# Cross-attention and MoE in one program on one core: the low-half matmuls moved last, VectorE's small steps moved behind the projection's sum, and two low halves moved behind the maxima

## The reference, cut to what matters

```python
q = (layernorm(x) @ Wq); k = context @ Wk; v = context @ Wv      # per head
attn = softmax(q @ k.T * SCALE)
x = x + (attn @ v) @ Wo + bo
h = layernorm(x)                      # then a routed MoE: 32 experts, top 4 of 2 groups of 4, and a shared one
x = x + mixed_experts(h) + shared(h)
```

## Time and profile before

| | |
|---|---|
| time, median of 3 runs | 3259.04 us (3258.24 to 3260.62) |
| the profiled execution's own time | 3257.45 us |
| its span, first to last instruction | 3255.6 us, granted clock 0.995 |
| attention's groups | to about 2952 us of the span; then the MoE |
| PE, DVE, ACT, POOL busy | 98%, 80%, 65%, 41% of the span |
| the chain that ended last | PE 85%, DVE 12% |

### The profile page before, as it was taken

The page is one execution under the profiler, slowest core; times in us unless marked ns, Lnnn a source line. Parts: engine busy times, 40 slices in busy tenths (PEclk is TensorE's granted clock), DMA queues, the critical chain, the costliest instruction groups (busy, mean ns, idle before and its releaser), DMA issues.

```text
span 3255.6 us, 39933 instructions
## 1 busy us (share of the span) xinstructions
PE 3185.7 (98%) x14510; PEld 2470.6 (76%) x14510; DVE 2619.5 (80%) x4840; ACT 2128.3 (65%) x2642; POOL 1327.1 (41%) x893
## 2 busy tenths in 40 slices
PE   7899999999999999999999999999999999999999
PEld 5677777777777777777777777777777777776787
DVE  5788888888888878888888888887888888888766
ACT  4566666666666666666666666666666666676555
POOL 4334433344334433344433434334433344225565
PEclk9999999999999999999999999999999999999999
DMA  2000000000000000000000000000000000115453
GB/s 82 6 27 11 15 22 6 27 11 27 11 22 11 27 11 11 22 11 27 11 27 6 27 11 11 27 6 27 11 27 11 22 11 11 50 26 115 112 131 76
DMA packets 52696, 93.13 MB, mean 29 GB/s; under 512 B 23699, under 2 KB 24468, under 8 KB 52116
## 3 DMA queue, kind: packets, MB, share of 16 engines
q1 hardware_dynamic: 52500, 90.58, 10.3%
HBM read 86.88 MB, written 2.88 MB: 28 GB/s over the span
## 4 chain that ended last, share of the span: by engine, by line
PE 85%; DVE 12%; issue 1%; ACT 1%; POOL 0%; DMA 0%; POOLq 0%; DVEq 0%; ACTq 0%
PE side L598 12%; PE st L658 11%; PE st L660 11%; PE st L663 10%; PE op L671 9%; PE op L677 9%; PE op L674 9%; DVE p_lo L1253 2%; DVE m_part L1270 2%; PE st L799 2%; PE st L801 2%; PE st L800 2%; DVE o_all L1121 1%; DVE o_all L1114 1%; PE side L591 1%
## 5 line engine op out<-in xcount | busy, mean ns | idle before, releaser
L530 POOL TENSOR_TENSOR p_lo<-p_full,p_hi 128x1024 fp32r<-128x1024 f32 x320 | 810.3, 2532 | 1788.7 <-ACT p_hi L963 1788.7
L1270 DVE TENSOR_REDUCE m_part<-side 128x1 f32<-128x400 f32 x2016 | 1073.7, 569 | 345.5 <-PE side L598 330.0
L960 ACT ACTIVATE p_full<-st 128x1024 f32<-128x1024 f32 x768 | 786.8, 1024 | 482.4 <-PE st L663 467.4
L963 ACT ACTIVATE p_hi<-st 128x1024 fp32r<-128x1024 f32 x768 | 784.3, 1021 | 0.0
L598 PE MATMUL side<-cT_hi,qT_hi 96*128 96x400 f32 x2016 | 597.2, 357 | 2.0
L1253 DVE TENSOR_TENSOR p_lo<-p_full,p_hi 128x1024 fp32r<-128x1024 f32 x448 | 546.2, 1219 | 35.6 <-ACT p_hi L963 34.3
L658 PE MATMUL st<-qT_hi,cT_hi 97*128 97x512 f32 x1664 | 536.0, 403 | 6.8 <-DMA qT_hi<-m_row 6.6
L660 PE MATMUL st<-qT_lo,cT_hi 96*128 96x512 f32 x1664 | 524.8, 396 | 0.0
L598 PEld LDWEIGHTS side<-cT_hi,qT_hi 96*128 96x128 f32 x2016 | 379.3, 188 | 165.1 <-DVE m_part L1270 61.8
L671 PE MATMUL op<-p_hi,v_hi 128*97 128x512 f32 x1536 | 488.0, 399 | 10.5 <-DVE p_lo L1253 7.4
L677 PE MATMUL op<-p_hi,v_lo 128*97 128x512 f32 x1536 | 481.5, 395 | 0.0
(11 more groups left out here) (180 smaller groups left out, 3385.0 us busy)
## 6 DMA issues: line engine op xcount, KB each, us to landing
w_rep<-w_rows SPq DMA_DIRECT2D x64, 512.0 KB, 6.7
r_rep<-r_rows SPq DMA_DIRECT2D x64, 384.0 KB, 3.1
keys_nat<-in_ctx_keys SPq DMA_DIRECT2D x16, 672.0 KB, 6.0
keys_tur<-in_ctx_turned SPq DMA_DIRECT2D x16, 600.4 KB, 4.8
gud_raw<-in_moe_w SPq DMA_DIRECT2D x2, 1152.0 KB, 9.1
out_x<-x SPq DMA_DIRECT2D x8, 256.0 KB, 2.0
x<-in_x SPq DMA_DIRECT2D x1, 1920.0 KB, 13.3
qT_hi<-m_row SPq DMA_DIRECT2D x64, 4.0 KB
```

The lines of the kernel that those rows point to most:

```text
L530: pool.tensor_tensor(p_lo[:, slot(s), :], p_full[:, (g * S + s) % 2, :], p_hi[:, slot(s), :].bitcast(F32), ALU.subtract).then_inc(s_lo_poo ...
L960: act.activation(p_full[0:m, now, :], made, ACT.Exp, scale=SCALE)
L963: act.activation(p_hi[0:m, slot(s), :], made, ACT.Exp, scale=SCALE).then_inc(s_ex, 1)
L1270: dve.tensor_reduce(m_part[:, k % NT, k // NT:k // NT + 1], where[:, 0:MAXW], AX.X, ALU.max).then_inc(s_drain, 1)
```

## The change

1. `weigh` orders its matmuls hi x hi, v_lo x p_hi, v_hi x p_lo. `wait_rest`, the wait for the low half, stands ahead of the last two only; at the start `weigh` waits for ACT's `p_hi`.
2. DVE drains Z and both Q directly behind `lo(12)`. `batch_stats` or `late_steps` come behind them, and `early_steps` of a group behind `lo(0)` of the next one.
3. In steps 2 and 3 DVE drains the step's second side jobs ahead of `lo(t - 1)`.
4. Step 6 has one M ahead of `weigh` and two behind (before: two and one), on PE and DVE.

```diff
-        PLACES = {... 6: ("MM", "M"),
+        PLACES = {... 6: ("M", "MM"),
...
-            def weigh(s, par):
+            def weigh(g, s, par):
...
                 for j in range(2):
-                    pe.matmul(op[0:OW, j, :], v_hi[par][:, tile, :], p_lo[:, slot(s), halves[j]],
+                    pe.matmul(op[0:OW, j, :], v_lo[par][:, tile, :], p_hi[:, slot(s), halves[j]],
                               start=False, stop=False)
+                wait_rest(pe, g, s)
                 for j in range(2):
-                    mm = pe.matmul(op[0:OW, j, :], v_lo[par][:, tile, :], p_hi[:, slot(s), halves[j]],
+                    mm = pe.matmul(op[0:OW, j, :], v_hi[par][:, tile, :], p_lo[:, slot(s), halves[j]],
                                    start=False, stop=(s == S - 1))
...
-                    wait_rest(pe, g, s)
                     if s == HALF:
+                        wait_rest(pe, g, s)
                         weigh_half(par)
                     else:
-                        weigh(s, par)
+                        pe.wait_ge(s_ex, n + s + 1)
+                        weigh(g, s, par)
...
                 lo(0)
+                if g:
+                    early_steps(g - 1)
                 for t in range(2, S):
                     if t == S - 1:
                         lo(t - 1)
                         lo(t)
-                        if i == 1:
-                            batch_stats()
-                        elif g:
-                            late_steps(g - 1)
-                        side_jobs(at[t][0])
...
+                    elif t > 3:
+                        side_jobs(at[t][0])
+                        lo(t - 1)
                     else:
                         side_jobs(at[t][0])
+                    if t < S - 1:
+                        side_jobs(at[t][1])
+                    if t <= 3:
                         lo(t - 1)
-                    side_jobs(at[t][1])
...
                 side_jobs(at[S - 1][2])
-                early_steps()
+                if i == 1:
+                    batch_stats()
+                elif g:
+                    late_steps(g - 1)
                 if g == NG - 1:
+                    early_steps(g)
                     late_steps(g)
```

More of the change, by code:

```diff
@@ L236, in xattn_moe @@
         both = lambda t: t.rearrange("p a b -> p (a b)")
-        PLACES = {2: ("MM", "MM"), 3: ("MM", "M"), 4: ("MM", "MM"), 5: ("MM", "M"), 6: ("MM", "M"),
+        PLACES = {2: ("MM", "MM"), 3: ("MM", "M"), 4: ("MM", "MM"), 5: ("MM", "M"), 6: ("M", "MM"),
                   7: ("MM", "MM"), 8: ("MM", "MM"), 9: ("MM", "MM"), 10: ("MM", "M"), 11: ("", "T"),
@@ L1291, in side_jobs, with tokens_of @@
                             queries_lo(where, 2 * g + 4 + k + 1, k, i % 2)
+                def tokens_of(batch):
+                    return [2 * batch + q for q in (4, 5, 0, 1)]
                 def batch_stats():
@@ L1298, in batch_stats, with early_steps @@
                     last_stats(tiles, 0)
[L1300 to L1306, removed]
+                def early_steps(group):
+                    batch, place_in_batch = divmod(group, NGB)
+                    those = tokens_of(batch)
+                    if place_in_batch == 0:
+                        first_stats(those[:2], 0)
+                    elif place_in_batch == 1:
+                        normalise(those, 0, batch + 2)
+                    elif place_in_batch == 2:
                         strike()
@@ L1318, in late_steps @@
                         route_scores()
-                tiles = [2 * b + q for q in (4, 5, 0, 1)]
+                tiles = tokens_of(b)
                 at = places(g)
                 lo(0)
+                if g:
+                    early_steps(g - 1)
                 for t in range(2, S):
```

## The result

| | before | after |
|---|---|---|
| median | 3258.81 us of 4 runs (3258.24 to 3260.62) | 3321.41 us of 4 runs (3312.93 to 3325.23) |
| ratio | | 1.0188, interval 1.0175 to 1.02 |
| profiled execution, span | 3257.45, 3255.6 us | 3325.23, 3323.4 us |
| granted clock | 0.995 | 0.992 |

A forecast was written before the change was run, and what follows sets the result against it. PE, busy 98% of the span, was taken as the bound; 3257.45 - 17.3 - 23.4 - 9.7 - 1.4 + 38.6 + 114.3 = 3358.5, the median 1.6 above: 3360 us, 3.1% slower, range 3266 to 3380.

The forecast's parts named there:

- `lo(2)` behind POOL's low half of tile 3: Step 3: DVE's `lo(2)` starts under POOL's operation and is held, PE waits in 63 groups, +114 us.
- POOL is first by 0.06: Step 3, after a third and a fourth group: POOL starts at T + 4.24, `lo(2)` at T + 4.30.
- the case held likeliest: POOL starts ahead of `lo(2)` in all kinds of group: 3360 us, own range 3335 to 3378, chance 0.60.
- rival 2: POOL first in the third kind and one or two others, an escaping kind saves 30: 3300 to 3330, chance 0.13.
- The price of a block held: PE's wait in a group when `lo(2)` is held: 1.9, 1.9, 1.6 and 1.9 us by kind.
- The small steps: Step 2: DVE's small steps ahead of the first M drains make PE wait, +38.6 us (22.6 with the bound).
- Step 12: Low half wanted four matmuls later, so a 0.27 us wait goes in 64 groups: -17.3 us.
- Q: Q's second half, written to Z's bank, waits only 0.14 us in all kinds: -23.4 us.
- Step 6: One M ahead of `weigh(4)` and two behind: the M pair's wait goes, 0.02 left at steps 7 and 8, -9.7 us.
- the prediction's list of what would be seen: Profile signs: `lo` of 3.5 us in each group, 1.5 us `p_lo` waits, L475 1 us later, no step 12 wait.

The follow-up runs named there:

- Experiments 2 to 4: The change's kernel plus: POOL waiting for `lo(2)`, 3257.32 us; a 128-element memset on DVE ahead of `lo(2)`, 3355.33; on POOL ahead of its tile 3 subtraction, 3277.33.
- Experiment 9: Part 2 of the change alone, in the kernel before: 3289.21 us, ratio 1.0096.
- Experiment 6: Part 1 of the change alone, in the kernel before: 3255.79 us, ratio 0.9988.
- experiments 1 and 10: 1: the change with `lo(2)` back ahead of step 3's drains, 3255.5 us; 10: also late small steps between Z's and Q's drains, early at group's end, 3192.78.

## Why the prediction was right, and where it was off

**The mechanism that decides was right.** The prediction named `lo(2)` behind POOL's low half of tile 3 as the deciding term. Experiments 2 to 4 show it as a cause: without the collision 64 us go, and a memset on either side moves the time by +34 or -44 us.

**Off: how many groups it takes.** The step "POOL is first by 0.06" was worked out from rows of 0.01 us each and was off by 0.03 to 0.07: the measured lead is 0.03 us or nothing in first groups and at most 0.01 in fourth ones. The prediction knew that its margins were small and still priced 63 blocks; there were 7 + 16 + 16 + 1 = 40. The 23 that escaped, at the 1.9 us that it gave a block of these kinds, are 44 us, about the distance from 3360 to 3321. Of the 40, the five late ones of the third kind cost 0.2 us each, and the clock took about as much as that saved. So the case held likeliest (POOL first in all kinds, 0.60) did not come; rival 2 (the third kind and one or two others blocked, 0.13, 3300 to 3330) did, nearly. The direction and the mechanism were reasoned. How many near ties would escape was not: with margins of hundredths of a microsecond the range took in all, some or none of them, and where in it the time fell was luck.

**The price of a block held: right.** Predicted 1.9, 1.9, 1.6 and 1.9 us by kind; measured 1.97, 2.0, 1.76 and 1.93 where the clock stayed up. The five late groups of the third kind are outside this (0.2 each).

**The small steps: right.** Predicted waits 1.61, 0.98, 1.27 and 0 behind a second, third, fourth and first group; measured 1.69, 0.93, 1.16 and 0.04. `rstd` is held by `lo(0)` (1.80 us, predicted about 2), and `var_eps`, `g_keep` and `w_new` are short, both as said. Experiment 9 has costs of the same size without the collision at `lo(2)`: 3.8 us more in a batch, as was expected of it.

**Step 12: the size right, its independence wrong.** The wait is 0 after the change. But the term was written as if it stood alone. Experiment 6 shows that alone most of it turns into a wait at Q, in three of the four kinds; beside part 2 both waits are gone. The sum was about right (46 us measured for the two, 41 predicted) because both were in it.

**Q: mis-sized.** Its floor is 0.07 us in all kinds, not 0.14, worth 4.5 us. Step 6: 7 us, not 9.7.

**Not foreseen: the clock.** Long waits of PE were priced at their length. Behind some of them the granted clock fell to half. By the lower clock's 20.9 us more, each at double the time of a matmul, this is some 10 us of PE's time; some 8 of them are in five second groups, and in four third groups a shorter block took the cost back. Why it falls behind these waits and not behind the others of the same length is open. The change's runs lie 12 us apart and those of before 2.4, and the clock does not explain it: the runs of 3325.23 and 3324.73 us had 0.992 and 0.993, the faster ones of 3312.93 and 3318.1 us had 0.990. Near ties that end otherwise, at 1.9 us each, would do it as well; only one of the four runs has a trace, so the cause is open.

By the prediction's list of what would be seen: the `lo` of about 3.5 us are there, but in 23 groups and not in each (17 more are held for less); the loads of the last matmuls wait 1.6 to 1.9 us where they do (1.5 predicted); POOL's L475 is 1 us longer; and the rows for step 12, Q and the small steps are as it says.

## What to carry to other kernels

Where two engines that hold each other off start within a few hundredths of a microsecond, read both starts and both lengths from the trace for every group: a working from rows of 0.01 us did not tell the outcome here, but one semaphore or one instruction's place fixes it (64 us here). A boundary between two starts holds only for the same instructions ahead of them (0.011 to 0.019 us in the change, 0.142 to 0.143 behind a memset). Price a moved instruction together with the engine that it frees or fills: a wait that one part removes came back at the next place until another part took the cause away (-4 alone, +16 alone, -16 together). Here the small steps belonged where their own engine waits for another one, not merely behind the urgent work: 63 us lie between experiments 1 and 10.

## What was not expected of the hardware

- In the change DVE started up to 0.011 us behind POOL and still went first; 0.019 behind, it was held until POOL's 2.4 us were over. The difference decides over 2.2 us of DVE and 1.9 of PE. With a memset ahead of `lo(2)`, starts up to 0.142 us behind still went first.
- A held instruction of DVE runs between two instructions of POOL, and the second of them pays: L475 took 2.25 us instead of 1.28.
- The granted clock was at 0.50 for some 3.4 us behind nine of PE's waits of 1.3 to 1.6 us, beginning 1.2 to 2.2 us after it had gone on (four matmuls of 512 columns then took 1.71 us by their starts, 1642.04 to 1643.75, and not 0.93), and did not fall behind some twenty others as long. The same stretch cost 1.6 us in second groups and nothing in third ones, where it kept `lo(2)` away from POOL's low half.
